# Moving an accumulating addition from TensorE to VectorE, moving one convolution in TensorE's order, and leaving the choice of ScalarE's function tables to the compiler

## The reference

```python
def _mamba(x, W_in, W_conv, b_conv, W_x, W_dt, b_dt, A_log, Dp, W_out):
    xp, z = jnp.split(x @ W_in.T, 2, axis=-1)
    xc = silu(causal_conv4(xp) + b_conv)            # 4 taps, per channel, 512 channels
    dt, Bm, Cm = jnp.split(xc @ W_x.T, [16, 32], axis=-1)
    dt = jax.nn.softplus(dt @ W_dt.T + b_dt)
    h = h * jnp.exp(dt * A) + (dt * u)[:, :, None] * B[:, None, :]   # per token, 16 states a channel
    y = jnp.einsum('bdn,bn->bd', h, C)
    y = (y + xc * Dp) * silu(z)
    return y @ W_out.T
xn = layernorm(h0, ln_w, ln_b)
mixed = h0 + 0.5 * (_mamba(xn, f_...) + flip(_mamba(flip(xn), b_...)))   # forward + backward
x = x + ga * mixed
x = x + gb * experts(layernorm(x) * (1 + cb) + sb)    # top 2 of 8 experts, and a shared expert
```

## Time and profile before

| | |
|---|---|
| median of three runs | 2238.33 us |
| the profiled execution | 2238.26 us, of which the span of the trace 2236.5 us |
| DVE busy | 2047.3 us (92%), 2381 instructions |
| PE busy | 1847.3 us (83%), 6152 matmuls |
| POOL busy | 1811.6 us (81%) |
| ACT busy | 1342.3 us (60%) |
| mean granted clock of TensorE | 0.874 of full speed |

### The profile page before, as it was taken

One profiled execution on the slowest core, in us unless ns is written; L12 is line 12 of the kernel. 1 busy time (PEld: TensorE's weight loads), 2 busy tenths in 40 slices (PEclk: granted clock), 3 DMA queues, 4 the chain that ended last, 5 costly groups with the idle time before them and its releaser, 6 DMA issues.

```text
span 2236.5 us, 24275 instructions
## 1 busy us (share of the span) xinstructions
PE 1847.3 (83%) x6152; PEld 765.3 (34%) x6153; DVE 2047.3 (92%) x2381; ACT 1342.3 (60%) x2404; POOL 1811.6 (81%) x652
## 2 busy tenths in 40 slices
PE   7687887878797879788787878797956699999997
PEld 3222332323232323233232323231312366655554
DVE  7899999999999999999999999999999877557776
ACT  3566757585766757675758576666755343424443
POOL 3389999999999999999999999999999434325444
PEclk9777988989898979798898989797967799999999
DMA  7734434343434344353534353444434462235554
GB/s 285 227 89 106 121 102 123 96 112 106 113 106 112 107 115 115 100 121 101 125 94 115 103 120 105 105 109 119 96 89 134 161 237 102 83 86 83 79 80 67
DMA packets 136494, 259.95 MB, mean 116 GB/s; under 512 B 19984, under 2 KB 42768, under 8 KB 135232
## 3 DMA queue, kind: packets, MB, share of 16 engines
q1 hardware_dynamic: 120064, 230.78, 38.8%
q0 software_dynamic: 13440, 17.93, 4.8%
q10 hardware_dynamic: 2880, 9.96, 1.1%
HBM read 190.32 MB, written 69.34 MB: 116 GB/s over the span
## 4 chain that ended last, share of the span: by engine, by line
DVE 47%; PE 22%; issue 14%; POOL 5%; ACT 4%; DMA 3%; DVEq 3%; SPq 1%; POOLq 0%; ACTq 0%
DVE hst L1364 30%; DVE dbu L1350 9%; PE psum L1764 4%; PE psum L1889 4%; POOL hst L810 3%; PE psum L1708 3%; PE psum L1722 2%; PE psum L1901 2%; PE psum L1752 2%; DVEq L1598 1%; DVE h L1608 1%; PE psum L1689 1%; DVE h L1620 1%; DMA b_rep<-bc_scratch 1%; ACT psum L1102 1%
## 5 line engine op out<-in xcount | busy, mean ns | idle before, releaser
L810 POOL TENSOR_TENSOR hst<-hst,c_rep 128x2048 f32<-128x2048 f32 x255 | 1152.1, 4536 | 22.6 <-ACT state L1090 20.1
L1102 ACT ACTIVATE psum<-dt_rep,neg_a 128x512 f32<-128x512 f32 x1024 | 692.8, 684 | 442.8 <-DVE hst L1364 433.8
L1364 DVE TENSOR_TENSOR_SCAN hst<-psum,state,dbu 128x512 f32<-128x512 f32 x768 | 919.3, 1257 | 0.0
L1350 DVE TENSOR_TENSOR dbu<-psum,b_rep 128x2048 f32<-128x2048 f32 x192 | 434.8, 2265 | 17.3 <-PE psum L1752 12.8
L1752 PE MATMUL psum<-dt,same 32*128 32x512 f32 x384 | 253.0, 743 | 192.8 <-DVE dbu L1350 184.5
L1764 PE MATMUL psum<-hst,same 128*32 128x512 f32 x2048 | 311.4, 763 | 50.3 <-POOL hst L810 42.0
L798 POOL TENSOR_TENSOR dbu<-dtu_rep,b_rep 128x2048 f32<-128x2048 f32 x64 | 291.7, 4558 | 45.8 <-DVE hst L1364 45.8
L1364 DVE TENSOR_TENSOR_SCAN hst<-psum,dbu 128x512 f32<-128x512 f32 x256 | 291.1, 1198 | 0.7 <-ACT psum L1102 0.7
L1708 PE MATMUL psum<-xp,taps 128*128 128x512 f32 x512 | 246.6, 632 | 5.6 <-ACTq L1019 4.8
L930 POOL DMA_INDIRECT out_x<-h,target_u x72 | 113.2, 1572 | 156.9 <-DMA out_x<-h,target_u 77.5
L1752 PEld LDWEIGHTS psum<-dt,same 32*128 32x128 f32 x384 | 64.9, 208 | 339.6 <-DVE dbu L1350 255.7
(11 more groups left out here) (175 smaller groups left out, 2236.8 us busy)
## 6 DMA issues: line engine op xcount, KB each, us to landing
dt_rep<-dt_scratch SPq DMA_DIRECT2D x256, 256.0 KB, 4.7
taps<-taps_scratch SPq DMA_DIRECT2D x64, 256.0 KB, 2.9
b_rep<-bc_scratch SPq DMA_DIRECT2D x64, 256.0 KB, 5.0
c_rep<-bc_scratch SPq DMA_DIRECT2D x64, 256.0 KB, 8.0
dt_scratch<-dt SPq DMA_DIRECT2D x64, 256.0 KB, 2.0
dtu_rep<-dtu_scratch SPq DMA_DIRECT2D x256, 64.0 KB, 1.9
h<-slot_scratch SPq DMA_DIRECT2D x72, 129.5 KB, 2.1
sp_tmp<-t_scratch SPq DMA_DIRECT2D x16, 512.0 KB, 4.9
```

The costliest lines, as they stand in the source:

```text
L810: nc.gpsimd.tensor_tensor(h, h, c_rep[q % 2][:], ALU.mult).then_inc(prod_done, 1)
L1102: nc.scalar.activation(psum[:, PS_A + i, :], dt_rep[:, G % 2, j, :], ACT.Exp, scale=neg_a[:, q % 2, u, i:i + 1]).then_inc(exp_done, 1)
L1350: nc.vector.tensor_tensor(dbu[:, U % DBU, :, :], psum[:, PS_U:PS_U + 1, :].broadcast_to((P, NG, TB)), b_rep[U // UNITS % 2][:], ALU.mult). ...
L1364: nc.vector.tensor_tensor_scan(time_order(hst[:, U % RING, i, :], backward), time_order(psum[:, PS_A + i, :], backward), time_order(dbu[:, ...
```

## The change

Four edits. (1) The identity matmul of `t_blk` goes from `project_out`; the sum is instead taken by a new DVE operation, `add_out`, which adds the PSUM bank to `t_blk` in place. (2) `copy_out` goes from ACT. `add_out` stands on DVE after the second scan of unit 3 (first half of the block) and of unit 4 (second half); for step 15 it stands after `norm_apply(0)` and after `norm_statistics(1)`. The wait for `t_blk`'s load moves with it from PE to DVE. (3) The naming of the table set goes, so that the compiler sets the loads. (4) `convolve(q+1, 2)` is issued by PE at the start of unit 4, ahead of `spread_input`, and no longer at its end.

```diff
--- before.py
+++ after.py
@@ -64,14 +64,11 @@
 
 XP_AT = [(15, 0), (15, 2), (3, 0), (3, 2)]
 CONV_AT = [(2, 1), (2, 2), (5, 1), (6, 0)]
-OUT_AT = [(4, 1), (5, 0)]
 SILU_X_AT = (6, 3)
 Z_AT = [(7, 1), (7, 3), (8, 1), (8, 3)]
 SILU_Z_AT = (8, 3)
 XDBL_AT = (9, 1)
 DT_AT = [(11, 0), (11, 1), (11, 3), (13, 2)]
-
-EXP_AND_LN = "natural_log_exp_and_others"
 LOG_AT = [(11, 3), (13, 3)]
 LOG_PART = [slice(0, NC - 1), slice(NC - 1, NC)]
 FIRST_LOG = [slice(0, 1), slice(1, NC)]
@@ -1027,16 +1024,11 @@
                 bank, free = filled(act, "z", q, c)
                 nc.scalar.activation(sz[:, c, :], psum[:, bank, :], ACT.Copy).then_inc(free, 1)
 
-            def copy_out(q, b):
-                bank, free = filled(act, "out", q, b)
-                nc.scalar.activation(t_blk[:, b * TB:(b + 1) * TB], psum[:, bank, :], ACT.Copy).then_inc(free, 1)
-
             def silu_z(q):
 
                 for c in (NC - 2, NC - 1):
                     drained(act, "z", q, c)
                 nc.scalar.activation(sz[:], sz[:], ACT.Silu).then_inc(sz_done, 1)
-                nc.scalar.preload_act_table_set(EXP_AND_LN)
 
             def copy_conv(q, c):
                 if c == 0 and q >= 2:
@@ -1140,8 +1131,6 @@
                     decay(T, n)
                     if T == 0 and n == 3:
                         copy_block(LAST)
-                    if q > 0 and (t, n) in OUT_AT:
-                        copy_out(q - 1, OUT_AT.index((t, n)))
                     if (t, n) in Z_AT:
                         copy_z(q, Z_AT.index((t, n)))
                     if (t, n) == SILU_Z_AT:
@@ -1203,11 +1192,8 @@
                                      batch_flag[:, n // SEG:n // SEG + 1, :].broadcast_to((P, NT, BATCH)), ACT.Copy
                                      ).then_inc(scaled, 1)
 
-            copy_out(STEPS - 1, 0)
             for n in range(NBLK):
                 turned(n)
-                if n == 0:
-                    copy_out(STEPS - 1, 1)
                 if n > 0:
                     scale_tokens(n - 1, 0)
                     silu_shared(0, n - 1)
@@ -1341,6 +1327,14 @@
                 dve.wait_ge(chunk_summed, NC * q + c + 1)
                 dve.wait_ge(sz_done, q + 1)
                 nc.vector.tensor_tensor(sz[:, c, :], psum[:, PS_Y, :], sz[:, c, :], ALU.mult).then_inc(yg_done, 1)
+
+            def add_out(q, b):
+
+                if b == 0:
+                    dve.wait_ge(t_loaded, 16 * (q + 1))
+                bank, free = filled(dve, "out", q, b)
+                dst = t_blk[:, b * TB:(b + 1) * TB]
+                nc.vector.tensor_tensor(dst, dst, psum[:, bank, :], ALU.add).then_inc(free, 1)
 
             def multiply(U):
 
@@ -1515,6 +1509,10 @@
                     if i == 1:
                         if t == 2 and q > 0:
                             gate_y(q - 1, 3)
+                        if t == 3 and q > 0:
+                            add_out(q - 1, 0)
+                        if t == 4 and q > 0:
+                            add_out(q - 1, 1)
                         if t == 10:
                             gate_y(q, 1)
                         if t == 14:
@@ -1531,7 +1529,9 @@
                 nc.vector.memset(mask[:, half, NT, :], 0.0).then_inc(mask_clear, 1)
             gate_y(STEPS - 1, NC - 1)
             norm_apply(0)
+            add_out(STEPS - 1, 0)
             norm_statistics(1)
+            add_out(STEPS - 1, 1)
             shift_logits(0)
             norm_apply(1)
             rank_experts(0)
@@ -1712,16 +1712,14 @@
             def project_out(q, b):
 
                 if b == 0:
-                    pe.wait_ge(t_loaded, 16 * (q + 1))
                     pe.wait_ge(yg_done, NC * (q + 1))
                 bank, full = take_bank(pe, "out", q, b)
-                nc.tensor.matmul(psum[:, bank, :], ident[:], t_blk[:, b * TB:(b + 1) * TB], start=True, stop=False)
                 for half in range(2):
                     tok = slice((2 * b + half) * P, (2 * b + half + 1) * P)
                     for c in range(NC):
                         ins = nc.tensor.matmul(psum[:, bank, half * DM:(half + 1) * DM],
                                                sz[:, c, tok], w_out[:, q % 2, c, :],
-                                               start=False, stop=(half == 1 and c == NC - 1))
+                                               start=(c == 0), stop=(c == NC - 1))
                 ins.then_inc(full, 1)
 
             def project_xdbl(q):
@@ -1804,6 +1802,8 @@
                         convolve(q + 1, 1)
                     if t == 2:
                         project_x(q + 1, 2)
+                    if t == 4:
+                        convolve(q + 1, 2)
                     if t == 5:
                         convolve(q + 1, 3)
                     if t == 8:
@@ -1834,8 +1834,6 @@
                     project_x(q + 1, 3)
                 if t == 3 and q > 0:
                     project_out(q - 1, 1)
-                if t == 4 and ahead:
-                    convolve(q + 1, 2)
                 if t == 6:
                     project_z(q, 1)
                 if t == 7:
```

## The result

The kernel after takes 2257.67 us (median of four runs, 2253.45 to 2262.47) against 2238.3 us before on the same chip: a ratio of 1.0087, 95% interval 1.0063 to 1.011. A second measurement on another chip gives 1.0083 (1.0066 to 1.01). It is slower, as forecast, but by 19 us and not by 9, and above 2256, the top of the range.

The account below looks back on a forecast made before the run. VectorE was taken to bound the loop, busy 1644.8 of 1657.5 us. Additions 17.4, new waits 1.0, old waits -7.3, step 0 -1.4, tables 1.1, tail -1.8 gave +9.0: 2247.3 us, range 2241.5 to 2256.

Parts of the forecast that it names:

- The additions: VectorE in the loop: 30 additions at 0.58 us each cost 17.4 us.
- grows by anything but 1.2 us: Sign that the forecast is wrong: an ordinary step, expected 1.16 us longer, grows by another amount.
- The wait for the output projection: VectorE's additions wait for TensorE's output in light steps 1, 8 and 9: 1.0 us in total.
- The five old waits: VectorE's waits for TensorE's spread_input in steps 1, 2, 8, 9 and 10 all go: -7.3 us.
- What is late next is VectorE itself: In the loop, with TensorE 3.0 us earlier relative to VectorE, no TensorE wait follows the removed ones.
- Step 0: First step, order change only: new 2.0 us wait, but old waits go; gains 1.4 us.
- The table loads: ScalarE's loads around each Ln delay decays 0.27 us in four light steps, nothing in the other eleven: +1.1 us.
- Rival (b): Table loads reach the scans in every step, 0.5 us each: +7.5 us, 2255 us; 13%.
- The prologue: Before the loop, four loads in ScalarE's softplus are hidden by idle time: 0, at most 1 us.
- Behind the loop: After the loop, step 15's two identity matmuls leave the chain that ends last: -1.8 us.
- Rival (c): A table load costs ScalarE twice its row, as the skill's rule says: 2306 us; 2%.
- Rival (a): Not slower: TensorE causes VectorE's gaps, and freeing it gives nearly everything back: 2241 us; 11%.

Follow-up runs that it names:

- e2: Kernel before with VectorE's additions replacing identity matmul and ScalarE copies, table set named and convolution at its old place: 2249.12 us, 1.0044.
- e4: Changed kernel with the table set named again, so all edits but the table loads: 2247.97 us, 1.0038 against before.
- e5_fill: Changed kernel with four overwritten matmuls added ahead of the second z projection, in TensorE's idle time: 2252.79 us, 1.0073 against before.
- e1_tables: Kernel before with only the naming of the table set taken out, so the compiler places the loads: 2248.95 us, 1.0051.
- e9: Changed kernel run again, unedited; its profile is the second profile of after: 2255.29 us, 1.0083 against before.
- e15: Kernel before without table naming, unit 11's state copy moved ahead of unit 12's first decay: 2241.46 us, 1.0014.
- e16: Changed kernel with unit 11's state copy moved ahead of unit 12's first decay: 2255.44 us, 1.0086 against before.
- e7: Kernel before with the spread of unit 8 issued in unit 5, ahead of the chunk sum: 2224.67 us, 0.9943.

## Why the prediction was wrong

- **The additions** were right: 0.585 us each against 0.58, and 1.17 us a step. The ordinary steps without a wait in the second profile of after (2, 3, 4, 10, 11 and 12) are 105.1 to 105.4 us, against 104.0 to 104.2 for those of before. In the first profile, with the new waits, ordinary steps are 105.5 to 106.3, and that is the sign "grows by anything but 1.2 us" that I had named.
- **The wait for the output projection**: 0.82 and 0.76 us in steps 1 and 9 where I had 0.4; none in step 8. 1.6 against 1.0. In the second profile it is 3.0 us in six steps, among them 0.28 in step 5, for which I had computed 1.9 us of room.
- **The five old waits** went, all 7.3 us. But "What is late next is VectorE itself" failed: the next is the spread of unit 9, and then the Silu of z. I followed TensorE, which becomes earlier, to the old wait and no further, to the place where it then waits for ScalarE and works more slowly behind the gap. "The moved convolution changes nothing in the sum of that work" left out the idle time ahead of the spread of unit 6 that the convolution fills; e2, without the move, has no late spread of unit 9, and e4, with it and with no loads, has it in 9 steps. e5_fill shows that the gap is the cause, and that it is worth 2 to 3 us.
- **Step 0** gained 1.1 us where I had 1.4, by luck. The new wait of 2.0 us that I had put in the sum did not come: the clock was full from 22 us of the step on, in before from 33; the two old waits, 3.4 us, did go, and the 1.35 us at that early product and new waits of 0.75 and 0.28 took most of it back. In the second profile step 0 gained 3.6. I had also left two waits of step 0 out of my list, 1.14 and 0.52 us.
- **The table loads** were the step that failed by most. "I find 0 to 0.3 us of room: nothing" looked at the scans alone. At unit 12 the scans do wait, 0.28 us where I had 0.27, four times; that close it is by luck, since the rows of the prediction give 281.96 + 0.68 - 282.46 = 0.18. I did not list what else stands behind the returning load in ScalarE's queue. It is the state copy, and it holds up an engine busy for 1588.6 of 1657.5 us. 1.1 against 10 to 11 us (by the ratios of e1_tables, and of after and e9 against e4), of which e15 shows the way of 7 to 8 in the kernel with this edit alone. The profiled executions show less of it in after: 2256.75 and 2251.19 us against 2250.45 for e4. Rival (b) had a cost in every step, and 7.5 us for it, but by the scans; the falsifier that I named for it, waits in unit 12 or 14 of ordinary steps, did not occur.
- **The prologue**: 0, at most 1; it is 2.5 in the profile of after, and the load at the first decays is not on the way to the first scan. All of it can be scatter: the first scan comes at 99.4 to 102.7 us in the profiles of kernels with that load (e16 has the 99.4) and at 99.6 to 101.3 in those without.
- **Behind the loop**: 2.1 us of the 3.8 lie ahead of the first `fmax`, and the identity matmuls are 1.96 of them (I had 1.8). The rest is within the scatter there.
- **Rival (c)**, a load at twice its row, is refuted. The Trainium skill, "ScalarE: Activation LUTs", section "What ACT_TABLE_LOAD costs", states a drain of about 1380 ns on top of the load. The trace doesn't agree, on either side of the load: the load at 596.25 starts 0.02 us behind the end of Exp (595.60 + 0.63), Ln starts 0.02 us behind its load (596.25 + 1.28, 597.55), and the decays 0.01 behind theirs (599.05 + 1.28, 600.34).
- **Rival (a)**: the relief of TensorE does give the old waits back, and e7 shows that a kernel that gains them and pays nothing for it is 13 us faster. After gets them back too, and loses about as much at the next places.

Why after loses about 10 us to the loads when the copy's place alone doesn't return them (e16) isn't settled by these runs.

## What to carry to other kernels

When an engine's instruction becomes slower, list everything queued behind it on that engine, however small, and for each who waits for it, before pricing the ones that the bound engine reads. When a wait is removed, walk the released engine on to its next wait and ask what its earlier arrival and a later partner make of that one: a wait that goes is only worth its row if none stands behind it. Work moved into an idle time does not remove that time: look where it comes back. And treat an engine that is 96% busy, as GpSimd is here, as bound too: a gap of 2.15 us ahead of its work became one of 1.66 us for the engine behind it.
